# Attention with rotary embedding and a mixture of experts on one core: sine rows exchanged inside SBUF instead of projected, whole pieces of 512 columns, norms in pairs

## The reference, cut to what matters

```python
def attn(x, Wq, Wk, Wv):                 # x: (4, 1024, 128), 16 heads of 8
    q, k, v = heads(x @ Wq.T), heads(x @ Wk.T), heads(x @ Wv.T)
    cos, sin = rope_tables(N, D)
    q = q * cos + rotate_half_interleaved(q) * sin     # pairs: (-x1, x0)
    k = k * cos + rotate_half_interleaved(k) * sin
    attn = softmax(einsum('bhnd,bhmd->bhnm', q, k) * scale)
    return einsum('bhnm,bhmd->bhnd', attn, v)

def ffn(x, ...):                          # 8 experts, top 2, hidden 256
    gate = softmax(x @ gate_w + gate_b)
    vals, idx = top_k(gate, 2)
    h = gelu(x @ w1[e] + b1[e]); h = gelu(h @ w2[e] + b2[e])
    y[e] = h @ w3[e] + b3[e]
    return sum(vals * y[idx])

xn = layernorm(x)
out = x + attn(xn, Wq, Wk, Wv) + ffn(xn, ...)
```

## Time and profile before

| | us |
|---|---|
| runs | 667.2, 670.16, 666.25; median 667.2 |
| the profiled execution | 665.8 |
| its span (first to last instruction) | 664.1 |
| mean granted clock of PE | 0.99 |
| busy PE, ACT, DVE, POOL | 619.4, 559.2, 243.4, 222.0 |

### The profile page before, as it was taken

The page is one execution under the profiler, slowest core; times in us unless marked ns, Lnnn a source line. Parts: engine busy times, 40 slices in busy tenths (PEclk is TensorE's granted clock), DMA queues, the critical chain, the costliest instruction groups (busy, mean ns, idle before and its releaser), DMA issues.

```text
span 664.1 us, 12748 instructions
## 1 busy us (share of the span) xinstructions
PE 619.4 (93%) x4234; PEld 271.1 (41%) x4234; DVE 243.4 (37%) x699; ACT 559.2 (84%) x626; POOL 222.0 (33%) x235
## 2 busy tenths in 40 slices
PE   8689999999999999888999999998999999999995
PEld 5223432322232222222888888883222222222221
DVE  5573346552232332202555555550203021220304
ACT  3689898899999999999555555558999999999995
POOL 2501013317767766540122211224242333324300
PEclk9799999999999999999999999998999999999999
DMA  7793014323433333396333433421122121112204
GB/s 218 198 388 112 18 47 144 112 80 127 138 125 124 123 119 119 127 283 164 64 76 71 79 71 71 87 52 41 51 72 72 40 72 55 55 48 79 63 9 131
DMA packets 84057, 68.56 MB, mean 103 GB/s; under 512 B 47280, under 2 KB 61136, under 8 KB 84016
## 3 DMA queue, kind: packets, MB, share of 16 engines
q1 hardware_dynamic: 77328, 53.78, 27.6%
q0 software_dynamic: 5968, 13.51, 6.6%
q10 hardware_dynamic: 720, 0.71, 0.4%
HBM read 33.51 MB, written 33.42 MB: 101 GB/s over the span
## 4 chain that ended last, share of the span: by engine, by line
PE 56%; ACT 21%; issue 13%; DVE 5%; DMA 2%; POOL 1%; ACTq 1%; SPq 0%; POOLq 0%; DVEq 0%
ACT probs L610 14%; PE ps L1192 13%; PE ps L1215 10%; ACT probs L576 7%; PE ps L1177 6%; PE ps L1225 5%; PE ps L1208 5%; PE ps L1298 5%; PE ps L1145 4%; PE ps L1282 3%; PE ps L1201 2%; PE ps L1110 1%; DVE xn_all L684 1%; DMA q_st<-parts 1%; DMA b_raw<-in_L_ffn_b_dram 1%
## 5 line engine op out<-in xcount | busy, mean ns | idle before, releaser
L576 ACT ACTIVATE probs<-ps 128x1024 f32<-128x1024 f32 x288 | 273.4, 1032 | 18.3 <-PE ps L1177 12.8
L610 ACT ACTIVATE probs<-ps 128x1536 f32<-128x1536 f32 (+1 forms) x154 | 202.1, 1447 | 0.9 <-PE ps L1282 0.8
L1192 PE MATMUL ps<-probs,v_st 128*32 128x512 f32 x1152 | 154.3, 608 | 12.2 <-ACT probs L576 8.5
L591 ACT ACTIVATE work<-ps,work 128x256 f32<-128x256 f32 x156 | 70.7, 475 | 65.6 <-PE ps L1215 65.1
L1298 PE MATMUL ps<-probs,v_st 128*32 128x512 f32 x896 | 120.5, 611 | 0.6 <-ACT probs L610 0.6
L513 POOL DMA_INDIRECT work<-slots_y_d,slot_i x64 | 60.4, 944 | 117.0 <-PE ps L1298 64.3
L1282 PE MATMUL ps<-q_st,k_st 32*128 32x512 f32 x448 | 77.7, 497 | 13.9 <-ACT probs L610 13.1
L1177 PEld LDWEIGHTS ps<-q_st,k_st 32*128 32x128 f32 x576 | 28.0, 183 | 128.7 <-ACT probs L576 100.1
L1177 PE MATMUL ps<-q_st,k_st 32*128 32x512 f32 x576 | 73.6, 500 | 6.8 <-DMA q_st<-parts 3.9
L1282 PEld LDWEIGHTS ps<-q_st,k_st 32*128 32x128 f32 x448 | 29.1, 182 | 119.9 <-ACT probs L610 108.8
L473 POOL DMA_INDIRECT slots_x_d<-xn_all,slot_i x64 | 62.1, 971 | 46.7 <-PE ps L1192 32.0
(11 more groups left out here) (147 smaller groups left out, 448.4 us busy)
## 6 DMA issues: line engine op xcount, KB each, us to landing
k_d<-parts SPq DMA_DIRECT2D x8, 1024.0 KB, 5.6
q_d<-parts SPq DMA_DIRECT2D x8, 1024.0 KB, 4.9
q_st<-q_d SPq DMA_DIRECT2D x30, 256.0 KB, 3.0
k_st<-k_d SPq DMA_DIRECT2D x30, 256.0 KB, 2.8
slots_x_d<-parts SPq DMA_DIRECT2D x5, 1024.0 KB, 11.7
work<-slots_x_d SPq DMA_DIRECT2D x80, 64.0 KB, 2.3
slots_y_d<-work POOLq DMA_DIRECT2D x39, 128.0 KB, 2.2
parts<-in_L_ffn_w_dram SPq DMA_DIRECT2D x16, 128.0 KB
```

The source lines that it names most:

```text
L576: nc.scalar.activation(probs[:, j % PROB_RING, 2 * pair:2 * pair + 2, :], score_slot(j, pair).rearrange("p (h n) -> p h n", h=2), ACT.Exp, ...
L591: ins = nc.scalar.activation(dst[:, par, k, :], src[k][:, 0:ST], ACT.Gelu, bias=b12_st[:, par, n, k:k + 1])
L610: nc.scalar.activation(group_probs(phase, g)[:, 0:size, :], group_slot(g)[:, 0:size * HALF].rearrange("p (h n) -> p h n", n=HALF), ACT.Exp ...
L1192: ins = nc.tensor.matmul(o_ps[32 * h:32 * h + 32, :], v_st[:, mt, h, :], probs[:, j % PROB_RING, h, :], start=(mt == 0), stop=(mt == MT - 1))
```

## The change

- The swap projections of batches 1 to 3 go. DVE multiplies the plain piece by cosine into t_cos and by minus sine (a table stored for the exchanged rows' places) into rot; SP then moves odd rows to even places and even to odd with two transfers from rot to t_sin (exchange_rows), and join_parts makes the high part three blocks after the projection. POOL's rotate also waits for the exchange.
- A piece is projected at once: 512 columns, one job instead of four.
- Norms go in pairs (key and query piece), in f32 instead of F32R, each into 32 columns of the array; one reduction on DVE reads both. Squares and head_r become f32.
- Values of batches 1 to 3 are projected two tiles a job. The places of all jobs are made by a new plan_jobs.
- prepare_batches becomes prepare_rows(b): batch 1 where it was, batches 2 and 3 at (0,11) and (1,3).
- The five clears of slots_x_d (1 MB each) move from the start to t = 1.
- The scatter's places come from plan_scatter: from block 59, every second or third block, never in a block with a join; the last pair at block 136.
- In the prologue a 64-column matmul on zeros follows each of eight transposes, four matmuls of 512 columns (WARM_AGAIN) stand before the first scores, and the first key load is split (128 columns first).
- The routing's exponential on ACT moves from the start of step 2 to its block 2, and the pieces of ROUTE move by a few blocks.

Places of the new plan, by block number: norm pairs 0 to 7 at 7, 16, 44, 53, 70, 82, 91, 102; rows of batch 1 at 10 and 11, of batch 2 at 18 and 19, of batch 3 at 24 and 26; values at 12 to 15, 20 to 23, 27 to 30; pieces 4 to 15 at 32, 35, 39, 43, 58, 63, 68, 74, 79, 84, 90, 95; joins three blocks after each; the count at 46; turns as before at j = 1 and j = 9 of each step.

```diff
 
...
+    return range(3 * n, min(3 * n + 3, BT)) if b == 0 else range(2 * n, 2 * n + 2)
+
+
 def plan_jobs():
...
-            (1, 5): ("rows", 3, 0), (1, 6): ("rows", 3, 1), (1, 7): ("values", 3, 0), (1, 8): ("values", 3, 1), (1, 10): ("values", 3, 2),
...
-            jobs[place] = job
+    turns = {BLOCKS * t + MT + 1 for t in range(SPLIT)} | {BLOCKS * t + 1 for t in range(1, SPLIT)}
+    fixed = {0: ("values", 0, 2), 7: ("norm", 0), 16: ("norm", 1), 46: ("count",), BLOCKS * 7 + 12: ("bound",)}
+    joins = {}
+
+    def place(job, n):
+        while n in turns or n in fixed:
+            n += 1
+        fixed[n] = job
+        return n
+    for b, n in ((1, 10), (2, 18), (3, 24)):
+        for half in range(2):
+            n = place(("rows", b, half), n) + 1
+        for k in range(BT // 2):
+            n = place(("values", b, k), n) + 1
+    for g, n in enumerate((32, 35, 39, 43), 4):
+        joins[place(("plain", g), n) + 3] = g
+    place(("norm", 2), 44)
+    place(("norm", 3), 53)
+    n = 55
+    for g in range(8, 16):
+        n = place(("plain", g), n + 2) + 3
+        joins[n] = g
+        if g % 2:
+            place(("norm", g // 2), n + 4)
+    jobs = {divmod(n, BLOCKS): job for n, job in fixed.items()}
     for t in range(SPLIT):
         jobs[(t, MT + 1)] = ("turn", t, 0)
         if t:
             jobs[(t, 1)] = ("turn", t - 1, 1)
-    return jobs
-
...
 AUX = {job: n for n, job in enumerate([JOBS[p] for p in sorted(JOBS)] + [("turn", SPLIT - 1, 1)])}
-ROUTE = {(1, 11): 0, (2, 0): 1, (2, 2): 2, (2, 3): 3, (2, 4): 4, (2, 5): 5, (2, 6): 6, (2, 7): 7, (2, 10): 8, (2, 13): 9, (2, 14): 10,
-         (2, 15): 11, (3, 2): 12, (3, 3): 13, (3, 4): 14, (3, 5): 15, (3, 6): 16, (3, 7): 17, (3, 10): 18}
+ROUTE_EXP = (2, 2)
+ROUTE = {divmod(block, BLOCKS): n for n, block in enumerate((31, 35, 36, 37, 38, 39, 42, 43, 45, 47, 50, 51, 52, 53, 54, 55, 58, 59, 60))}
...
+    joins = [t * BLOCKS + j for t, j in JOINS]
+    starts, n = {}, max(t * BLOCKS + j for t, j in ROUTE) - 1
+    for i in range(TILES):
+        while n in joins or n in starts:
+            n += 1
+        starts[n] = i
+        n += 2 + (i % 3 == 2)
+    return starts
...
-            first_load(0, S["ka_loaded"])
+            first_load(0, S["k00_loaded"], 0, P)
+            first_load(0, S["ka_loaded"], P, HALF)
...
             store_parts(3)
-            for r in range(SLOT_ROOM // 8):
-                sp.dma_start(slots_x_d[r * 8 * ST:(r + 1) * 8 * ST, :].rearrange("(p a j) c -> p a (j c)", p=P, a=4),
-                             parts[:, :, 3, :].bitcast(F32)).then_inc(S["x_zeroed"], 16)
...
+            def exchange_rows(g):
+
+                u = g % 2
+                sp.wait_ge(S["aux_read"], AUX[("plain", g)] + 1)
+                sp.wait_ge(rot_made[u], g // 2)
+                sp.wait_ge(hi_made[u], g // 2)
+                for odd in range(2):
+                    sp.dma_start(t_sin[odd:P:2, u, :], rot[1 - odd:P:2, u, :]).then_inc(exchanged[u], 16)
...
-                    g = swaps.get(divmod(t * BLOCKS + j - 2, BLOCKS))
+                    if t == 1 and 2 <= j < 2 + SLOT_ROOM // 8:
+                        r = j - 2
+                        sp.wait_ge(S["scores_done"], t * UNITS + 2 * j)
+                        sp.dma_start(slots_x_d[r * 8 * ST:(r + 1) * 8 * ST, :].rearrange("(p a j) c -> p a (j c)", p=P, a=4),
+                                     parts[:, :, 3, :].bitcast(F32)).then_inc(S["x_zeroed"], 16)
+                    g = JOINS.get(divmod(t * BLOCKS + j - 2, BLOCKS))
                     if g is not None:
                         store_parts(g)
+                    job = JOBS.get((t, j), ("none",))
+                    if job[0] == "plain":
+                        exchange_rows(job[1])
...
+                if g >= 4:
+                    pool.wait_ge(exchanged[u], 32 * (g // 2 - 1))
...
-                    pool.wait_ge(S["aux_done"], AUX[("norm", g - 2)] + 1)
+                    pool.wait_ge(S["aux_done"], AUX[("norm", g // 2 - 1)] + 1)
...
-            starts = {3 * BLOCKS + MT + 5 * i // 2: i for i in range(TILES)}
+            starts = plan_scatter()
...
-                    job = JOBS.get((t, j), ("none",))
-                    if job[0] == "swap" and job[2]:
-                        pool.wait_ge(S["aux_read"], AUX[job] + 1)
-                        rotate(job[1])
-                        low_part(job[1])
-                        square(job[1])
+                    if (t, j) in JOINS:
+                        rotate(JOINS[(t, j)])
+                        low_part(JOINS[(t, j)])
+                        square(JOINS[(t, j)])
...
             with act.Fori(0, 2) as t:
                 attention_exps(t)
+            attention_exps(ROUTE_EXP[0], 0, 2 * ROUTE_EXP[1])
             act.wait_ge(S["max_made"], 1)
             nc.scalar.activation(rt[:, 1], rt[:, 0], ACT.Exp).then_inc(S["exp_made"], 1)
-            with act.Fori(2, SPLIT) as t:
+            attention_exps(ROUTE_EXP[0], 2 * ROUTE_EXP[1])
+            with act.Fori(3, SPLIT) as t:
                 attention_exps(t)
...
+            def peak(pair):
+
+                n = AUX[("norm", pair)]
                 dve.wait_ge(S["aux_done"], n + 1)
-                nc.vector.tensor_reduce(peaks[:, u, b, m:m + 1], aux_ps[0:16, :], AX.X, ALU.max).then_inc(S["aux_read"], 1)
...
+            def prepare_rows(b):
+
+                if b == 1:
+                    statistics(BT, TILES)
+                    invert_rest()
+                for k in range(BT):
+                    ins = normalise_row_tile(b * BT + k)
+                ins.then_inc(S["batch_rows_made"], 1)
...
+            def plain_part(g):
 
                 u, m = g % 2, g // 2 % 2
...
+                cols = slice(m * HALF, (m + 1) * HALF)
+                dve.wait_ge(S["aux_done"], AUX[("plain", g)] + 1)
...
+                nc.vector.tensor_tensor(t_cos[:, u, :], aux_ps, cos_sb[:, cols], ALU.mult)
+                dve.wait_ge(lo_made[u], g // 2)
+                dve.wait_ge(hi_made[u], g // 2)
+                dve.wait_ge(again_made[u], g // 2)
+                dve.wait_ge(sq_made[u], g // 2)
+                nc.vector.scalar_tensor_tensor(rot[:, u, :], aux_ps, -1.0, sin_sb[:, cols],
+                                               ALU.mult, ALU.mult).then_inc(S["aux_read"], 1)
+
+            def join_parts(g):
+
+                u = g % 2
+                dve.wait_ge(exchanged[u], 32 * (g // 2 - 1))
+                dve.wait_ge(parts_stored[g % 4], 16 * (g // 4))
+                nc.vector.tensor_tensor(high(g), t_cos[:, u, :], t_sin[:, u, :], ALU.add).then_inc(hi_made[u], 1)
...
-                            prepare_batches()
+                            prepare_rows(1)
...
+                    if (t, j) in JOINS:
+                        join_parts(JOINS[(t, j)])
+                    if (t, j) in ((0, 11), (1, 3)):
+                        prepare_rows(2 + t)
...
                 ins = nc.tensor.transpose(bank(k // 4)[:, (k % 4) * C:(k % 4 + 1) * C], xn_all[:, k, :], ident)
                 if k % 4 == 3:
                     ins.then_inc(S["trans_done"], 1)
+                nc.tensor.matmul(aux_ps[:, 0:C // 2], zeros[:, 0:P], zeros[:, 0:C // 2], start=True, stop=True)
...
+            def norm(pair):
+
+                n = AUX[("norm", pair)]
+                pe.wait_ge(S["aux_read"], n)
+                for u in range(2):
+                    pe.wait_ge(sq_made[u], pair + 1)
+                    ins = nc.tensor.matmul(aux_ps[32 * u:32 * u + 32, :], head_r[:], squares[:, u, :], start=True, stop=True)
+                ins.then_inc(S["aux_done"], 1)
...
+            def project(g):
+
+                b, lo = g // 4, g // 2 % 2 * HALF
+                free_aux(AUX[("plain", g)])
+                nc.tensor.matmul(aux_ps, weights(g, 0), xnT[:, b, lo:lo + HALF],
                                  start=True, stop=True).then_inc(S["aux_done"], 1)
...
+                    pe.wait_ge(S["ka_loaded"], t * 16 + 16)
...
+            for _ in range(WARM_AGAIN):
+                nc.tensor.matmul(bank(0), zeros[:, 0:P], xnT[:, 0, 0:HALF], start=True, stop=True)
             pe.wait_ge(S["proj_read"], 4)
             scores(0, 0, first=True)
```

133 lines of the change are left out of this document (44 added, 89 removed).

## The result

The changed kernel takes **670.9 us** (median of 10 runs, 668.9 to 672.0) where the kernel before took 667.5 (10 runs beside them): ratio 1.0049, interval 1.0034 to 1.0064. The interval is the 95% one. The forecast was 665.1 us, 0.3% faster; it is 0.5% slower, inside the range given and on the other side of no change. The profiled execution took 671.0 us, span 669.2; the one of before 665.8 and 664.1.

The account below looks back on a forecast made before the run. PE's side jobs laid over an ACT-bound loop were taken to set the first attention phase. Terms -1.3 -2.5 -0.6 +0.2 +2.1 sum to -2.1 us: profiled execution 663.7, median 665.1, range 658.0 to 671.5.

Parts of the forecast that it names:

- Start: Prologue and blocks 0 and 1: the added matmuls save 2.2 us, the zero matmuls cost 0.9; sum minus 1.3 us.
- The 0.9 for the zero matmuls: Prologue: zero matmuls set transposes 0.36 us apart instead of 0.26, plus 0.9 us, all on the path.
- Blocks 2 to 31: First attention phase: the rows job no longer waits, minus 2.3 us, with values, norms and prepare_rows; sum minus 2.5 us.
- Blocks 32 to 53: Stretch with four pieces, two norm pairs, token count, three turns and late copy_o; 46.3 us, minus 0.6.
- the stall of copy_o: Block 40: values wait for copy_o behind piece 6 and route 5 on DVE, plus 1.8 us.
- a free L833: Block 40: if route 5's L833 is not held up, the copy_o stall costs 0.8 us instead of 1.8.
- The collision of joins and sums: Joins on DVE and rotate on POOL would collide each time; copy_o at blocks 72 and 88 1.3 late, 2 us more.
- Blocks 54 to 119: Stretch with eight pieces, four norm pairs, eight turns and three late copy_o: 128.9 us, plus 0.2.
- In before the join: Exchange: two 128 KB transfers land in 3 to 4 us, before the join over 5.5 us later; no cost.
- Hand-over: Before layer 1: the later scatter on SP makes row loads 3.4 us late; plus 2.1 us, between 0 and 4.1.
- 1 (670.3 by the hand-over): SP's wait at (8,9): layer 1 starts 4.0 us late and PE's clock falls; 7.3 instead of 2.1; chance 0.16.
- 3 (norms one behind the other): Norm pairs: the two products do not overlap, 1.15 us a pair instead of 0.38, plus 6.2, 671.3; chance 0.10.

Follow-up runs that it names:

- run 2: Changed kernel with routing pieces moved to other blocks, none in 38, 39 and 47, ahead of a copy_o; 666.6 us, ratio 0.985 to the kernel before.
- run 7: Changed kernel with the norm pair in one-pass form, squares and head matrix F32R; 669.3 us, ratio 1.0028 to the kernel before.
- run 1: Changed kernel with POOL's four operations on each part of batch 1 on 8 columns instead of 512; 667.0 us, ratio 0.987 to the kernel before.
- run 6: Changed kernel with SP issuing each exchange one block later, behind that block's key and query loads; 675.4 us, ratio 1.011 to the kernel before.
- run 3: Changed kernel with the last two experts' weights loaded from blocks 8 and 9, ahead of SP's scatter wait; 670.9 us, ratio 0.992 to the kernel before.

## Why the prediction was wrong

- **Start, -1.3 forecast, -1.9 measured.** Right in the clock: it is 1.00 from 24.49 to 28.37, and blocks 0 and 1 take 1.8 us less (2.0 forecast). The 0.9 for the zero matmuls was too much: they set transposes 0.285 apart instead of 0.26 and cost 0.38 us. The first projections are 0.64 late, 0.26 of it because DVE's rows start later in this execution, but the first scores only 0.18 (23.86 against 23.68): the query load lands 4.2 us after its issue instead of 5.3. The forecast costed the split of the first key load at nothing; whether it is what made the query load quicker wasn't tested.
- **Blocks 2 to 31, -2.5 and -2.4.** Right in the rows job that no longer waits. The agreement is in part luck: the terms named add to -2.1, a norm pair costs 0.46 here and not 0.35, and what makes up for it is a term not named, two half projections of the kernel before that lie in this stretch (blocks 30 and 31: 2.06 and 2.13 us, where a light block takes 1.82).
- **Blocks 32 to 53, -0.6 and +4.4: the step that failed.** The term that failed is the stall of copy_o, 1.8 us at one place. The forecast saw copy_o of block 40 behind piece 6 and route 5, and priced it with route 5 at 1.0 to 1.5 us. It had the reason in its hand, L833 held up beside POOL's L431, but applied it to one routing piece and to joins against sums. It didn't apply it to routes 2, 3 and 4, which the new order of POOL's work, released by the exchange, puts beside L481 to L472; their four two-input operations, and not route 5 (0.51 us), were long (4.9 us where 1.7 would do), and DVE came late to piece 6 itself. Nor did it see the scans of route 9 ahead of block 48, and it gave the stall no clock. Measured against run 2: 3.9 us at block 40 where 1.8 was forecast, and 3.4 at block 48 where nothing was, 7.3 together; the fall of the clock is 1.5 of the second (run 7) and was not measured apart at the first. What the forecast says of a free L833, 0.8, is right: run 1 keeps 1.0. Without the stall its sum (44.5) is within 0.5 us of run 2.

  The rule that a DVE instruction with two SBUF inputs and a GpSimd one that reads SBUF lock each other out is stated by the Trainium skill (SBUF — State Buffer, section Who interferes with whom; the exclusive lock itself in section Terms). By that rule the trace agrees: run 1 takes POOL's work away and each of the four is 0.42 or 0.43. The collision of joins and sums that the forecast named went mostly the other way: eleven of the twelve joins take 0.67 to 0.69 us, one 1.20, and it is POOL's sum that is longer in five places (1.53 to 1.69 instead of 1.27).
- **Blocks 54 to 119, +0.2 and +2.3.** Terms too small: pieces 5.1 us instead of 4.4 (0.54 to 0.68 each; the 1.05 from start to the values is exact, less of it hides); norms 2.2 instead of 1.5 (five fall into the stretch, 0.46 each, not 0.38); turns with late copy_o 3.0 instead of 2.9; and the exchange, costed at nothing, holds SP: step 4's second key half is issued at 164.4 (162.1 in run 6, where it stands ahead), and the scores of block 67 wait for it.

```profile
162.42 1.90 SPq L372 DMA_DIRECT2D work<-work  x2
164.37 1.04 SPq L337 DMA_DIRECT2D k_st<-k_d  x1
...
168.54 0.51 PE L1225 MATMUL ps<-q_st,k_st 32*128 32x512 f32 x4 [0.74 <-DMA k_st<-k_d]
```

  "In before the join" was right in most places; what stands behind the exchange on its own queue was not asked.
- **Hand-over, +2.1 and +2.2.** The size is right and the place (SP's order). The forecast got its figure from late rows; run 3 shows that what ended last was the last expert's weights, behind the same wait, so the exact agreement is luck.
- **Rivals.** 1 (670.3 by the hand-over) gave nearly the time, by luck: layer 1 was no later than forecast. 3 (norms one behind the other) falls by the rows under run 7. None had DVE's queue. That the time lies in the range is luck too, since no case in it has these stalls. The list of what would show it wrong had joins waiting for the exchange; five of twelve do (7.5 us in all), mostly without cost to PE.

## What to carry to other kernels

Before work is moved on one engine, write out for each engine that others wait for what stands ahead of the awaited instruction there, with durations from the place where it will run, not from where it ran: two-input DVE work beside POOL took up to 3.3 times its time (1.39 us for 0.42). When a transfer is added to a queue, ask what is queued behind its wait. A routing piece that costs nothing behind the awaited copy cost several microseconds ahead of it, and a stall of PE costs more than its length when the clock falls behind it (3.4 us instead of 1.9 at block 48).
